# Attention value products in runs of nine steps instead of three, in a one-core fusion kernel

## The reference

```python
h = tok(x, W); h = concat([h, txt(x_txt, ...)], axis=1)        # (16, 1101, 128)
y = layernorm(h)
q, k, v = y @ wq, y @ wk, y @ wv                                # 8 heads of 64
o = softmax(q @ k.T / 8) @ v
h = h + concat_heads(o) @ head_kernel
z = layernorm(h) * ln_scale + ln_bias
shared = swiglu(z @ shared_in.T) @ shared_out.T + shared_bias
g = argmax(z @ group_gate.T); top2 = top_k(softmax(expert logits of group g), 2)
routed = cnt @ expert_bias + sum_e comb_e * (swiglu(z @ expert_in.T) @ expert_out_e.T)
out = h + shared + routed
```

## Time and profile before

| | |
|---|---|
| median of 3 runs | 4683.88 us (4683.44 to 4684.33) |
| profiled execution | 4684.45 us, span 4682.7 us |
| PE busy | 4476.3 us (96%) |
| POOL busy | 2943.6 us (63%) |
| DVE busy | 3215.6 us (69%) |
| ACT busy | 2298.7 us (49%) |

### The profile page before, as it was taken

One profiled execution on the slowest core, in us unless ns is written; L12 is line 12 of the kernel. 1 busy time (PEld: TensorE's weight loads), 2 busy tenths in 40 slices (PEclk: granted clock), 3 DMA queues, 4 the chain that ended last, 5 costly groups with the idle time before them and its releaser, 6 DMA issues.

```text
span 4682.7 us, 93178 instructions
## 1 busy us (share of the span) xinstructions
PE 4476.3 (96%) x26597; PEld 3324.5 (71%) x26597; DVE 3215.6 (69%) x7726; ACT 2298.7 (49%) x5640; POOL 2943.6 (63%) x1803
## 2 busy tenths in 40 slices
PE   5999999999999999999999999999999999999996
PEld 3667767777677776767777677776767777677765
DVE  5557767677675776768677675776767677686754
ACT  1555545445544555545545444555445455455441
POOL 0776666666666666666666666666666666666661
PEclk7999999999999999999999999999999999999998
DMA  2111111111101111111111111111011111111000
GB/s 53 35 34 41 33 30 40 39 25 34 45 24 39 32 32 40 30 33 40 33 32 34 32 37 39 25 34 45 25 38 35 30 39 34 30 40 37 21 21 19
DMA packets 157061, 159.01 MB, mean 34 GB/s; under 512 B 66576, under 2 KB 148359, under 8 KB 156551
## 3 DMA queue, kind: packets, MB, share of 16 engines
q1 hardware_dynamic: 156551, 152.68, 13.4%
HBM read 59.63 MB, written 19.65 MB: 17 GB/s over the span
## 4 chain that ended last, share of the span: by engine, by line
PE 84%; issue 4%; DVE 4%; DMA 3%; ACT 3%; POOL 1%; DVEq 0%; ACTq 0%; SPq 0%; POOLq 0%
PE o_ps L791 23%; PE work L688 12%; PE scores L772 12%; PE scores L774 11%; PE work L747 9%; PE work L680 4%; PE work L731 3%; PE work L673 2%; DMA sums<-inverse_rows 2%; PE work L708 2%; PE work L699 2%; PE work L736 1%; ACT probs L877 1%; DVE part_max L935 1%; POOL sums L1165 1%
## 5 line engine op out<-in xcount | busy, mean ns | idle before, releaser
L1165 POOL TENSOR_TENSOR sums<-sums,probs 128x736 f32<-128x736 f32 (+3 forms) x1344 | 2363.4, 1758 | 838.7 <-ACT probs L877 780.8
L877 ACT ACTIVATE probs<-scores 128x368 f32<-128x368 f32 (+3 forms) x3456 | 1460.2, 475 | 1542.5 <-PE scores L774 1487.1
L935 DVE TENSOR_REDUCE part_max<-work 128x1 f32<-128x368 f32 (+3 forms) x3456 | 1655.3, 530 | 449.5 <-PE work L688 439.1
L772 PE MATMUL scores<-q_a,k_a 128*128 128x368 f32 (+3 forms) x3456 | 1191.7, 345 | 84.0 <-issue 43.3
L791 PE MATMUL o_ps<-probs,values 128*64 128x368 f32 (+1 forms) x6912 | 1219.2, 489 | 1.6 <-ACT probs L877 0.2
L774 PE MATMUL scores<-q_b,k_b 128*128 128x368 f32 (+3 forms) x3456 | 1147.5, 332 | 0.0
L688 PE MATMUL work<-k_a,q_a 128*128 128x368 f32 (+3 forms) x3456 | 928.8, 352 | 9.1 <-DMA q_a<-q_b 8.1
L791 PEld LDWEIGHTS o_ps<-probs,values 128*64 128x64 f32 (+1 forms) x6912 | 453.0, 138 | 539.0 <-issue 447.1
L772 PEld LDWEIGHTS scores<-q_a,k_a 128*128 128x128 f32 (+1 forms) x3456 | 636.3, 184 | 200.4 <-ACT probs L877 77.9
L688 PEld LDWEIGHTS work<-k_a,q_a 128*128 128x128 f32 (+1 forms) x3456 | 595.0, 185 | 234.2 <-issue 208.8
L774 PEld LDWEIGHTS scores<-q_b,k_b 128*128 128x128 f32 (+1 forms) x3456 | 639.9, 185 | 17.4 <-issue 4.2
(11 more groups left out here) (183 smaller groups left out, 4493.1 us busy)
## 6 DMA issues: line engine op xcount, KB each, us to landing
sums<-inverse_rows SPq DMA_DIRECT2D x192, 184.0 KB
k_a<-k_a SPq DMA_DIRECT2D x128, 184.0 KB, 2.7
q_a<-q_b SPq DMA_DIRECT2D x128, 184.0 KB, 2.7
k_a<-k_a SPq DMA_DIRECT2D x64, 183.0 KB, 2.7
q_a<-q_b SPq DMA_DIRECT2D x64, 183.0 KB, 2.7
resid_rows<-heads_t SPq DMA_DIRECT2D x16, 576.0 KB, 6.2
h_out<-resid_rows SPq DMA_DIRECT2D x16, 576.0 KB, 8.0
heads_t<-in_pe_table_dram SPq DMA_DIRECT2D x16, 512.0 KB
```

What stands on the lines that cost most here:

```text
L772: nc.tensor.matmul(o, k_a[p % 2][i][:, t * P:t * P + n], q_a[p % 2][i][:, c0:c0 + cw], start=True, stop=False)
L877: nc.scalar.activation(probs[0:n, slot(s), i, 0:cw], scores[0:n, h % SB, 0:cw], ACT.Exp, scale=DH ** -0.5).then_inc(probs_ready, 1)
L935: nc.vector.tensor_reduce(part_max[0:n, i * IMG + j if j < IMG else 2 * IMG + i, c:c + 1], w[0:n, 0:keys], AX.X, ALU.max).then_inc(drained ...
L1165: nc.gpsimd.tensor_tensor(acc, acc, probs[0:n, slot(s), :, 0:cw], ALU.add).then_inc(sums_done, 1)
```

## The change

1. All nine steps of a block are multiplied by the values in one run (`GROUPS = (9,)`). A run stands where the table has `|`: at the end of step 8 of its block, and before the scores of the next block. Before, the third run of a block stood in the next block's step 0.
2. `probs` has eight buffers. The ninth step of a block uses the first step's buffer again. Its exponentials therefore wait until the first value products of the run are made, and the first step of the next block waits until those of the ninth are made and summed.
3. ACT rounds the queries into `q_a` itself. `q_b` is one buffer for all pairs. Its first 64 rows are filled by DMA from `q_a`, one chunk at the start of a block, once the old chunk is used up (`copy_q`). The maxima go into row 64 in two parts: the first two chunks after `r`, the third with the copy of the third chunk at the start of the next pair, four DMAs behind a new semaphore `max_loaded_late`. PE waits for a chunk of `q_b` at the first step of each block. An `m` unit waits for the keys' DMA alone.
4. The table of steps is written anew. It has the same units in the same order within each letter, at other steps.

```diff
+LAST0 = CHUNKS[-1][0]
-GROUPS = (3, 3, 3)
-NP = 2 * MOST - 1
+GROUPS = (9,)
+NP = 8
-BURST = ("burst",)
+FIRST_BAR = 0
 TIMETABLE = """
-|c/kuu/kuu/km|sm/mk/kmuu/m|m/mmmuu/mmmuu/
+c/ku/ukuku/mksm/mkm/mum/um/mmuu/mmmm|/
...
-def burst(s):
-    _, start, _, position = group_of((s - 1) % ALL)
-    if position < group_of((s - 1) % ALL)[2] - 1:
-        return []
-    start -= ALL if s == 0 else 0
-    return list(range(start, s))
+def burst(n):
+    start = n // len(GROUPS) * NT + sum(GROUPS[:n % len(GROUPS)])
+    return range(start, start + GROUPS[n % len(GROUPS)])

 def slot(s):
-    n, _, _, position = group_of(s)
-    return n % 2 * (MOST - 1) + position if position < MOST - 1 else NP - 1
+    return s % NT % NP
...
-                    pe.wait_ge(qk_again[what, part], 16 * (qk_pair(b, p) + 1))
+                    if what == "k":
+                        pe.wait_ge(qk_again[what, part], 16 * (qk_pair(b, p) + 1))
...
+            if t == 0:
+                pe.wait_ge(qk_again["q", c], 16 * (PAIRS * b + p + 1))
+            if s % STEPS == (NC - 1) * NT:
+                pe.wait_ge(max_loaded_late, 64 * (PAIRS * b + p + 1))
...
-                hi = k_a if what == "k" else q_b
+                hi = k_a if what == "k" else q_a
...
+        def copy_q(seg, b, q):
+            if not (seg.attn or seg.prep and q > (PAIRS - 1) * NC):
+                return
+            p, c = (q + NC - 1) // NC, (q - 1) % NC
+            if p == PAIRS and not seg.prep:
+                return
+            if seg.attn:
+                chunks_scored(b, q)
+            n = PAIRS * b + p
+            c0, cw = CHUNKS[c]
+            wait_then(sp.wait_ge, qk_hi, 12 * n + 4 * c + 4)
+            sp.dma_start(q_b[0:64, :, c0:c0 + cw].bitcast(F32),
+                         both_qa[p % 2][0:64, :, c0:c0 + cw].bitcast(F32)).then_inc(qk_again["q", c], 16)
+            if c == NC - 1:
+                max_rows_to_q_b(LAST0, TP, max_loaded_late)
...
+            if s % NT == 0:
+                copy_q(seg, b, s // NT)
```

More of the change, by code:

```diff
@@ L84 @@
 TIMETABLE = """
-|kk//k/km|sm/pkmm/pkm/pm|mm/pm/mmpmm/
-|pmmmm/pmm/pmm/mmpm|sm//mmm/m|mm/mmm/mmmmm/
-t|mmmm/tmmm/tmmm/mmm|sm/mg/rvv/|vv/vv/vk/
-|c/kuu/kuu/km|sm/mk/kmuu/m|m/mmmuu/mmmuu/
[L89 to L96, removed]
+k//k/skkmm/pkm/mpkm/pmmm/mmp/mpmmm|/
+pmm/mpmmm/pmm/mmpms//mmmm/mm/mm/mmmmm|/
+tmmm/mmmmt/mtmm/mmmmms/mg/vvvr//vvvkv/|/
+c/ku/ukuku/mksm/mkm/mum/um/mmuu/mmmm|/
+mummu/mmm/mu/mmms/mmumm/mmm/mmmu/mmm/mum|/
+mmm/mummmmm/mu/msmmm/mmu/uur/vv/uu/uuu|/
+u/kku/u/kksmu/mkm/mxk/memm/me/mmm|/
+mmm/uu/mm/mmmsm/mmmm/mmmumm/um/mmfm/mmufmmm|m/
+mmf/mmmm/mmm/smm/mmmmu/u/rv/vvvvuuv/vvk|/
+uv/u/kukuu/ks/mkum/mku/mmm/mm/ummmm|/
+mmm/mmmuu/mmmm/sm/mmmm/mmm/mu/mummm/mmumm|m/
+mmm/mmmu/mmm/smm/mm/m/r//|
 """.split("/")
@@ L183, in plan @@
             if letter == "|":
-                if attn and s > 0 or post and s == 0:
-                    units.append(BURST)
+                if attn and bar >= 0 or post and bar < 0:
+                    units.append(("burst", bar))
+                bar += 1
             else:
@@ L501, in fusion_kernel @@
     both_ka = [sb(ctx, f"k_a{r}", [P, 2, TP], F32R) for r in range(2)]
-    both_qb = [sb(ctx, f"q_b{r}", [P, 2, TP], F32R) for r in range(2)]
+    q_b = sb(ctx, "q_b", [P, 2, TP], F32R)
     q_a = [[both[:, i, :] for i in range(2)] for both in both_qa]
     k_a = [[both[:, i, :] for i in range(2)] for both in both_ka]
-    q_b = [[both[:, i, :] for i in range(2)] for both in both_qb]
     k_b = [[sb(ctx, f"k_b{r}{i}", [P, TP], F32R) for i in range(2)] for r in range(2)]
@@ L793, in weigh_one, with weigh @@
             mm.then_inc(probs_used, 1)
-        def weigh(seg, it, b, s):
-            for done in burst(s):
-                weigh_one(seg, it, b - (s == 0), done % ALL)
+        def weigh(seg, it, b, n):
+            for s in burst(n):
+                weigh_one(seg, it, b - (n < 0), s % ALL)
         def step(seg, it, b, s):
@@ L1165, in step @@
                 nc.gpsimd.tensor_tensor(acc, acc, probs[0:n, slot(s), :, 0:cw], ALU.add).then_inc(sums_done, 1)
-        for r in range(2):
-            for i in range(2):
-                ins = nc.gpsimd.memset(q_b[r][i][64:128, :].bitcast(F32), 0.0)
-        ins.then_inc(prepared, 1)
+        nc.gpsimd.memset(q_b[64:128, :, :].bitcast(F32), 0.0).then_inc(prepared, 1)
         pool.wait_ge(prepared, PREPARED)
@@ L1188, in seed, with chunks_scored, max_rows_to_q_b @@
             sp.dma_start(h_in[0:TXT, IMG, :], text_dram[n]).then_inc(seeded, 16)
+        def chunks_scored(b, q):
+            if not isinstance(b, int) or 2 * (ALL * b + q * NT) > 0:
+                wait_then(sp.wait_ge, scores_ready, 2 * (ALL * b + q * NT))
+        def copy_q(seg, b, q):
[13 more added lines that the diff above has]
+                max_rows_to_q_b(LAST0, TP, max_loaded_late)
+        def max_rows_to_q_b(first, end, loaded):
+            whole = range(-(-first // P), min(end // P, IMG))
+            for i in range(2):
+                target = q_b[64:65, i, whole[0] * P:(whole[-1] + 1) * P].bitcast(F32)
+                sp.dma_start(target.rearrange("p (a n) -> p a n", a=len(whole)),
+                             max_rows[i * IMG + whole[0]:i * IMG + whole[-1] + 1, :].bitcast(F32)).then_inc(loaded, 16)
+            j = LAST0 // P
+            part = slice(0, LAST0 % P) if end == LAST0 else slice(LAST0 % P, P)
+            sp.dma_start(q_b[64:65, :, j * P + part.start:j * P + part.stop].bitcast(F32),
+                         max_rows[j:IMG + j + 1:IMG, part].bitcast(F32)).then_inc(loaded, 16)
+            if end == TP:
+                sp.dma_start(q_b[64:65, :, HW:TP].bitcast(F32),
+                             max_rows[2 * IMG:2 * NT, 0:TP - HW].bitcast(F32)).then_inc(loaded, 16)
         def store_inverses(b, q):
@@ L1218, in step @@
             for u in seg.at[s]:
[L1219 removed]
+                if u[0] == "qk" and u[2] == "k":
                     _, p, what, c = u
                     c0, cw = CHUNKS[c]
[L1222 to L1225 removed]
+                    wait_then(sp.wait_ge, qk_hi, 12 * qk_pair(b, p) + 4 * c + 2)
+                    sp.dma_start(both_ka[p % 2][64:128, :, c0:c0 + cw].bitcast(F32),
+                                 both_ka[p % 2][0:64, :, c0:c0 + cw].bitcast(F32)).then_inc(qk_again[what, c], 16)
                 if u[0] == "maxrow":
                     wait_then(wait_drained, sp, seg, it, u)
[L1228 to L1232 removed]
+                    if seg.attn:
+                        chunks_scored(b, (u[1] - 1) % PAIRS * NC + NC - 1)
+                    max_rows_to_q_b(0, LAST0, max_loaded)
                 elif u[0] == "sum":
```

28 lines of the change are left out of this document (10 added, 18 removed).

## The result

| kernel | median us | runs | ratio to before, 95% interval |
|---|---|---|---|
| before | 4683.66 | 4 | |
| changed | 4731.96 (4727.94 to 4734.3) | 4 | 1.0102 (1.0085 to 1.012) |

A forecast was written before the change was run, and what follows sets the result against it. PE's instruction costs, one behind the other, were taken as the bound. Per item -8.2 + 4.8 - 1.5 = -4.9 us, over 16 items -78 us, so about 4606 us; range 4560 to 4668.

The forecast's parts named there:

- What bounds the kernel, and the switch: PE's instruction costs bound; 36 runs per item become 12, each saving 0.34 us, so 8.2 us per item.
- The waits at the banks and at ACT: New PE waits for free banks (1.3 us) and ACT without cover: 4.8 us per item, bounds 2 and 9.
- One `q_b`: Single query buffer filled by DMA: costed at nothing, 0.5 us per pair in the upper bound.
- The start of an item: 0.5 us back at step 0's `k` units, 1.0 us at step 9, where `p` waits for POOL's scaling.
- Eight buffers, and POOL: A block's first exponentials wait for POOL's sums, covered by the long run: costed at nothing.
- The branch and the clock: At the 13 item boundaries, PE's branch gap and the low clock behind it: both costs kept as they are.
- its signs of being wrong: DVE waits over 1 us in blocks from 36, 63, 90, or PE waiting while ACT waits for POOL's sums.
- rival A: The branch at item boundaries vanishes behind the long run: 74 us more gain, 4532 us; chance 0.06.
- B: DVE and ACT starve in the six blocks with most DVE work: +5.8 us per item, 4777 us; chance 0.12.
- C: Waits for DVE and ACT, 4 to 5 us above the sum, eat the gain: 4675 to 4694; 0.10 with D.
- the stated range: Range given for the changed kernel's time: 4560 to 4668 us; its own per-item working gave 4561 to 4673.

The follow-up runs named there:

- hid_lo_pool: Changed kernel with the gate chain behind the row copy, steps 54 to 61 and 81 to 83 nearly at old places, `hid_lo` on GpSimd: 4632.25 us.
- the adds cut: POOL's adds cut to 8 columns, softmax sums left out: 4664.09 us on the kernel before, 4631.04 us on the changed kernel.
- old_table_run9: Changed kernel with the old table's places for the units and one run of nine per block: 4840.07 us.

## Why the prediction was wrong

**What bounds the kernel, and the switch.** Right as far as it can be checked: the run takes 5.72 us where 5.7 was forecast, and begins 0.25 us behind the last score product. The 8.2 us per item, from 0.34 us per run read from the earlier trace rows, were not measured by themselves.

**The waits at the banks and at ACT.** This is the step that failed: 4.8 us per item, with the bounds 2 and 9, against some 13 (11.7 and the 1.5 that came back). The terms that it lists were near, though these measured ones are totals and were in part there before. In kernels where the meetings of DVE and POOL are gone, PE loses about 1.1 us in steps 30 to 33 of `hid_lo_pool` (forecast 1.5), 0.7 in steps 24 and 25 (0.9), and about 1.0 in steps 81 to 86 with the adds cut (1.1). What was missing was above all a mechanism. I gave every DVE instruction the duration of an undisturbed one. An instruction under a POOL add takes up to 1.6 us more, and the stretched time alone (100 to 141 us) doesn't show the price. PE loses 1.1 us per item to POOL's adds before and 7.0 after, of which 0.8 through POOL's late sums. I put the growth down to the runs of 2 us that let DVE catch up, and the old places of the units behind them, which are gone; the two were not told apart. The row was in reach: a `hid_lo` of 2.01 us beside one of 0.55, and in the earlier trace rows I looked only at maxima, which are never stretched.

That accounts for 5.9 of the 8.4 us between the forecast of -4.9 and the +3.47 per item. With the adds cut the item is 279.33 us, near the 278 to 279 of the forecast, but the kernel before also shortens, to 281.79. Like for like the change brings 2.5 us per item there, half of the 4.9. The idle time at the branch, 3.4 us on average in the one and 4.0 in the other, is part of what is left. The rest was not found.

**One `q_b`.** Costed at nothing; it is 28 us of gain by itself, mostly because POOL's adds and `hid_lo` change phase. A moved transfer needn't be on the path to move the time.

**The start of an item.** Right. Steps 0 to 2 lose some 1.0 us less with the adds cut (0.5 forecast), and the wait of `p` for POOL's scaling at step 9 is gone.

**Eight buffers, and POOL.** Costed at nothing, and wrong. What PE loses in step 9 is down only from 1.05 to 0.58 us, because a new wait stands there: ACT's first exponentials wait for POOL's sum of step 8. With step 10 and step 19 it costs 0.8 us per item, 13 us in all. The prediction named such a wait among its signs of being wrong. It took POOL's place in the run from POOL's adds alone, and left out that the scaling of the item before, which waits for its inverses, stands ahead of the sum in POOL's order. ACT waits 164.5 us for POOL's sums in the changed kernel and 45.1 in the one before.

**The branch and the clock.** Right to keep both. The idle time behind the run is 3.9 us at 1784.91, so rival A falls. Over the 13 boundaries it is 4.0 us on average (52.0 / 13), against 3.3 before, so this cost rose a little. The clock fell at the boundary as before; that it would also fall in block 2 was not foreseen (10 us in all).

**The rivals.** B has the sign, at twice the size (4777), but not its mechanism. It expected DVE's total work to run out of room in six heavy blocks, but in blocks 4, 7 and 10 PE loses at most 0.4 us more than before, and what blocks 3 and 6 lose goes mostly to single stretched instructions. C's sum is too small. And the stated range ends at 4668, where its own working gives 4673.

## What to carry to other kernels

Before a change takes the slack from behind an engine, compare the longest and the shortest duration of each of that engine's instructions. Where they differ by more than the slack that is left, find the instruction beside it. If VectorE operations with two SBUF inputs share their time with long GpSimd operations, give them to GpSimd as well, or put them behind what PE waits for; moving them by a step only changes which add they meet. And a table of steps that was fitted by measurement to one rhythm is part of that rhythm: neither half of such a change can be priced alone.

## What the runs showed that I had not expected

- A VectorE operation on 36 columns takes 0.20 us alone and 1.79 us beside a GpSimd add of 1.77, and both end together. With PSUM among the inputs none of 3467 was held.
- GpSimd's add of 16 elements per partition takes 0.22 us, of 184 0.58, of 368 0.98, of 736 1.77: a fixed part of some 0.2 us makes four pieces dearer than one by 0.6.
- 3.9 us of idle time at the loop's branch follow also a run of 5.8 us in which nothing waits. PE's sequencer does get ahead: the branch begins 3.1 us before the run ends, some 20 products early. But it then lasts 6.8 us in the median where it lasted 3.5 before. In `old_table_run9`, with the same run ahead of it, it lasts 4.0, PE idles 0.6 to 2.3 us at 12 of the 13 boundaries, and the granted clock behind them is 1.00 at 11. What sets its length is open. The branch in the changed kernel and in `old_table_run9` (columns as in the earlier trace rows):

```profile
L624 PEldq COMPARE_BRANCH  x14: 83/6754/6904, 630.1 to 4357.2; - x14
L624 PEldq COMPARE_BRANCH  x14: 83/3977/6616, 639.0 to 4452.2; - x14
```
